# A two-layer graph kernel with its normalised activations made a step ahead, in three buffers, and transposed by one DMA a step, all engine orders rewritten

## The reference

```
h = relu(layernorm(x))                              # over the 256 features
x = x + L0(h, adj, adj, bias)                       # A = adj @ h, C = adj @ h + b,
                                                    # out = max over features of relu(A + (C - A)[..., None])
h = relu(layernorm(x))
x = x + L1(h, ...)                                  # masked attention, 8 heads of 32
```

## Time and profile before

| | us |
|---|---|
| runs of the kernel | 1011.68, 1016.46, 1025.72; median 1016.46 |
| the profiled execution | 1012.4, its span 1010.7 |
| TensorE busy | 817.2 (81% of the span) |
| VectorE busy | 645.9 (64%) |
| ScalarE busy | 489.5 (48%) |
| GpSimd busy | 429.1 (42%) |
| mean granted clock of TensorE | 0.909 of full speed |
| DMA share, mean rate | 120 GB/s |

### The profile page before, as it was taken

The page is one execution under the profiler, slowest core; times in us unless marked ns, Lnnn a source line. Parts: engine busy times, 40 slices in busy tenths (PEclk is TensorE's granted clock), DMA queues, the critical chain, the costliest instruction groups (busy, mean ns, idle before and its releaser), DMA issues.

```text
span 1010.7 us, 31246 instructions
## 1 busy us (share of the span) xinstructions
PE 817.2 (81%) x11241; PEld 536.8 (53%) x11241; DVE 645.9 (64%) x1552; ACT 489.5 (48%) x1192; POOL 429.1 (42%) x853
## 2 busy tenths in 40 slices
PE   1578998788789888888987888798888889997862
PEld 0235665455556555555655555565555566654641
DVE  3554776666667666766765666686576677775653
ACT  3334555454455545545554444555454455553441
POOL 5411554344454434434544343454334445542343
PEclk9788998899999989989998998999899899998885
DMA  4466564667655676676556767555677755655313
GB/s 122 91 143 140 119 130 107 133 137 142 127 99 134 126 128 133 142 148 109 116 127 121 131 137 147 100 125 127 118 138 134 129 122 132 131 117 95 81 23 42
DMA packets 168295, 121.34 MB, mean 120 GB/s; under 512 B 84720, under 2 KB 167408, under 8 KB 167664
## 3 DMA queue, kind: packets, MB, share of 16 engines
q1 hardware_dynamic: 67328, 69.72, 27.2%
q10 hardware_dynamic: 83952, 33.04, 20.8%
q0 software_dynamic: 16896, 16.78, 11.2%
HBM read 35.06 MB, written 33.55 MB: 68 GB/s over the span
## 4 chain that ended last, share of the span: by engine, by line
PE 63%; DMA 17%; issue 9%; DVE 3%; SPq 3%; ACT 3%; POOL 2%; ACTq 1%; DVEq 0%; POOLq 0%
PE a_ps L319 20%; DMA hT<-h_lo 15%; PE sum_ps L446 8%; PE sc_ps L396 6%; PE pv_ps L416 6%; PE sum_ps L419 4%; PE a_ps L304 4%; PE sc_ps L368 4%; PE sc_ps L344 4%; SPq L273 2%; PE a_ps L332 2%; PE sum_ps L443 2%; ACT o_sb L590 1%; PE pv_ps L431 1%; ACTq L533 1%
## 5 line engine op out<-in xcount | busy, mean ns | idle before, releaser
L319 PE MATMUL a_ps<-hT,w_hi 128*128 128x512 f16 x512 | 170.6, 467 | 96.0 <-DMA hT<-h_lo 94.6
L844 POOL TENSOR_TENSOR oT_lo<-oT,oT_hi 128x256 f16<-128x256 f32 x128 | 84.6, 670 | 297.4 <-ACT oT_hi L584 297.3
L673 DVE TENSOR_REDUCE smax<-sc_ps 128x4 f32<-128x512 f32 x256 | 163.7, 681 | 51.7 <-PE sc_ps L368 51.6
L561 ACT ACTIVATE pairs<-a_ps 128x512 f16<-128x512 f32 x128 | 77.8, 608 | 231.1 <-PE a_ps L319 231.1
L665 DVE TENSOR_TENSOR pairs<-a_ps,pairs 128x512 f16<-128x512 f32 x128 | 87.3, 682 | 125.8 <-ACT pairs L561 125.8
L319 PEld LDWEIGHTS a_ps<-hT,w_hi 128*128 128x128 f16 x512 | 53.6, 115 | 168.2 <-issue 113.5
L838 POOL TENSOR_TENSOR h_lo<-h_sb,h_hi 128x256 f16<-128x256 f32 x128 | 89.1, 698 | 116.9 <-ACT h_hi L524 116.5
L571 ACT ACTIVATE p_sb<-sc_ps 128x512 f32<-128x512 f32 x256 | 137.1, 610 | 1.0 <-PE sc_ps L396 0.9
L578 ACT ACTIVATE pv_sb<-pv_ps 128x256 f32<-128x256 f32 x128 | 50.5, 394 | 146.2 <-issue 97.4
L416 PE MATMUL pv_ps<-p_sb,v_sb 128*32 128x128 f32 x2048 | 107.2, 278 | 6.1 <-ACT pv_sb L578 2.6
L723 DVE SCALAR_TENSOR_TENSOR t_sb<-o_sb,mv,w_sb 128x256 f32<-128x256 f32 x128 | 70.1, 586 | 60.9 <-POOL w_sb L869 60.9
(11 more groups left out here) (105 smaller groups left out, 1545.0 us busy)
## 6 DMA issues: line engine op xcount, KB each, us to landing
stack<-pairs SPq DMA_DIRECT2D x768, 64.0 KB, 2.0
out<-in_x SPq DMA_DIRECT2D x32, 512.0 KB, 4.2
out<-y_sb POOLq DMA_DIRECT2D x32, 512.0 KB, 8.4
x_sb<-in_x ACTq DMA_DIRECT2D x31, 512.0 KB, 3.6
stack<-crow SPq DMA_DIRECT2D x64, 8.0 KB, 1.9
w_sb<-in_L_gnn_w_qkv SPq DMA_DIRECT2D x1, 768.0 KB, 7.1
x_sb<-in_x SPq DMA_DIRECT2D x1, 512.0 KB, 3.7
hT<-h_hi ACTq DMA_TRANSPOSE x32, 6.3
```

The lines of the kernel that those rows point to most:

```text
L319: mm = nc.tensor.matmul(a_ps[c % 2][:].rearrange("p (b n) -> p b n", b=G), w[:, dc, col:col + P], hT[:, par, part, :, dc], start=(k == 0), ...
L673: nc.vector.tensor_reduce(smax[:, HC * j:HC * (j + 1), b], sc_ps[u % SC_SLOTS][:], AX.X, ALU.max).then_inc(smax_ready, 1)
L844: nc.gpsimd.tensor_tensor(oT_lo[:, b], oT[:, b], oT_hi[:, b], ALU.subtract).then_inc(olo_ready, 1)
```

## The change

h_hi and h_lo become two halves of one tile `h_parts` with three buffers (`SLOTS`), so what H0 waits for lies two steps further back. One DMA transposes both halves (16 blocks of 128 x 128 in place of 8 and 8), and `hT_in` counts 16 a step. x is normalised two groups ahead of the projections instead of one (a new flag, `norm`), with `rstd1` and `shift1` in three buffers, and it is loaded three groups ahead instead of two; the set-up normalises group 1 and loads group 2 before the pipeline starts. The orders of all five engines are rewritten.

```diff
-        h_hi = sb("h_hi", [P, G, D], F16)
-        h_lo = sb("h_lo", [P, G, D], F16)
+        h_parts = sb("h_parts", [P, SLOTS, 2, G, D], F16)
...
-                step(t, t % SLOTS, t < STEPS, 1 <= t <= STEPS, 2 <= t <= STEPS + 1, t >= 3, t + 1 < STEPS, t + 2 < STEPS)
+                step(t, t % SLOTS, t < STEPS, 1 <= t <= STEPS, 2 <= t <= STEPS + 1, t >= 3, t + 1 < STEPS, t + 2 < STEPS,
+                     t + 3 < STEPS)
...  SyncE
-            ORDER = ("Q0 M0 C0 Q1").split()
+            ORDER = ("C0 Q0 M0 Q1").split()
...  TensorE
-                    pe.wait_ge(hT_in, 32 * (t + 1))
+                    pe.wait_ge(hT_in, 16 * (t + 1))
...
-            ORDER = ("K0 S0 S1 S2 R0 S3 Q0 Q1 R1 N0 E0 E1 E2 L0 R2 E3 O0 R3 K1 S4 O1 L1 S5 S6 O2 S7 O3 Q2 M0 N1 E4 E5 "
-                     "P0 P1 E6 E7 P2 P3 Q3 P4 P5 V0 P6 P7 V1").split()
+            ORDER = ("K0 S0 S1 R0 S2 Q0 S3 R1 Q1 N0 E0 R2 O0 E1 E2 E3 L0 O1 R3 K1 S4 S5 O2 S6 S7 L1 O3 N1 M0 E4 E5 E6 "
+                     "P0 P1 Q2 P2 P3 Q3 P4 P5 E7 V0 P6 P7 V1").split()
...  ScalarE
-            def h_high(t, b):
+            def h_high(t, par, b):
                 act.wait_ge(h_ready, G * t + b + 1)
                 if b == 0:
-                    wait(act, a_psum, 2 * t)
-                    wait(act, hT_in, 32 * t)
-                nc.scalar.activation(h_hi[:, b], h_sb[:, b], ACT.Copy).then_inc(hhi_ready, 1)
+                    wait(act, a_psum, 2 * (t - 2))
+                    wait(act, hT_in, 16 * (t - 2))
+                nc.scalar.activation(h_parts[:, par, 0, b], h_sb[:, b], ACT.Copy).then_inc(hhi_ready, 1)
...
-                for part, h in enumerate((h_hi, h_lo)):
-                    nc.scalar.dma_start_transpose(hT[:, par, part].rearrange("p b c n -> p (b c) n"),
-                                                  h[:].rearrange("p b d -> p (b d)")).then_inc(hT_in, 16)
+                nc.scalar.dma_start_transpose(hT[:, par].rearrange("p a b c n -> p (a b c) n"),
+                                              h_parts[:, par].rearrange("p a b d -> p (a b d)")).then_inc(hT_in, 16)
...
                 wait(act, h_ready, G * (t - 2))
+                act.wait_ge(x_loaded, 16 * t)
                 nc.scalar.dma_start(x_sb[:, par], xg[t]).then_inc(x_loaded, 16)
...
-            ORDER = ("Q0 C0 X0 Q1 C1 E0 E1 E2 E3 C2 O0 C3 O1 R0 R1 H0 O2 R2 O3 H1 M0 H2 R3 A0 Q2 E4 E5 E6 A1 H3 E7 Q3 "
-                     "A2 T0 A3 V0 L0 V1").split()
+            ORDER = ("C0 Q0 R0 R1 C1 Q1 E0 C2 O0 E1 E2 E3 H0 O1 X0 C3 R2 O2 H1 H2 O3 R3 M0 H3 E4 A0 T0 Q2 A1 E5 Q3 E6 "
+                     "E7 A2 V0 A3 V1 L0").split()
...
-                        load_x(t + 2, (k + 2) % SLOTS)
+                        load_x(t + 3, k)
...  VectorE
-            ORDER = ("I0 I1 I2 S0 O0 S1 S2 S3 Q0 O1 X0 X1 O2 O3 Q1 L0 B0 S4 S5 B1 B2 S6 S7 B3 G0 M0 L1 F0 Q2 F1 Q3 F2 "
+            ORDER = ("I0 I1 I2 S0 O0 S1 S2 S3 O1 Q0 O2 X0 Q1 L0 B0 O3 S4 B1 S5 S6 S7 B2 B3 M0 X1 G0 L1 Q2 F0 Q3 F1 F2 "
                      "F3").split()
...
-                            stats_x(t + 1, (k + 1) % SLOTS)
+                            stats_x(t + 2, (k + 2) % SLOTS)
...  GpSimd
-            ORDER = ("C0 C1 X0 C2 C3 H0 H1 N0 H2 W0 W1 W2 H3 W3 K0 D0").split()
+            ORDER = ("C0 C1 C2 H0 C3 H1 H2 H3 N0 W0 W1 W2 W3 K0 D0 X0").split()
...
-                        invert_std_x(t + 1)
+                        invert_std_x(t + 2, (k + 2) % SLOTS)
```

More of the change, by code:

```diff
@@ L228, in pipeline @@
                 for k in range(SLOTS):
-                    step(t + k, (k + 1) % SLOTS, True, True, True, True, True, True)
+                    step(t + k, (k + 1) % SLOTS, True, True, True, True, True, True, True)
             for t in range(STEPS - SLOTS - 1, STEPS + SLOTS):
@@ L273, in stack_heads, with step @@
                         nc.sync.dma_start(dst.rearrange("p s b n -> p s (b n)"), src).then_inc(stacked[j], 16)
-            ORDER = ("Q0 M0 C0 Q1").split()
-            def step(t, k, a, sc, e, d, prep, load):
+            ORDER = ("C0 Q0 M0 Q1").split()
+            def step(t, k, a, sc, e, d, prep, norm, load):
                 for what in ORDER:
@@ L297, in _, with layer0 @@
             pe.wait_ge(dve_const, 3)
-            def layer0(t, i):
+            def layer0(t, par, i):
                 pe.wait_ge(qkhi_ready, 4 * t + i + 1)
                 pe.wait_ge(qklo_ready, 4 * t + i + 1)
-                for k, (w, h) in enumerate(((adjT_hi, h_hi), (adjT_hi, h_lo), (adjT_lo, h_hi))):
-                    mm = nc.tensor.matmul(a_ps[i][:], w[:], h[:, 2 * i:2 * i + 2].rearrange("p b d -> p (b d)"),
+                for k, (w, h) in enumerate(((adjT_hi, 0), (adjT_hi, 1), (adjT_lo, 0))):
+                    mm = nc.tensor.matmul(a_ps[i][:], w[:], h_parts[:, par, h, 2 * i:2 * i + 2].rearrange("p b d -> p (b d)"),
                                           start=(k == 0), stop=(k == 2))
@@ L819, in carry_waits, with invert_std_x @@
                 nc.gpsimd.tensor_tensor(pool_cell[:, cell:cell + 1], pool_cell[:, 0:1], pool_cell[:, 0:1], ALU.add)
-            def invert_std_x(t):
+            def invert_std_x(t, par):
                 pool.wait_ge(mv1_ready, G * (t + 1))
-                wait(pool, h_ready, G * t)
+                wait(pool, h_ready, G * (t - 2))
                 carry_waits(1)
```

44 lines of the change are left out of this document (24 added, 20 removed).

## The result

The changed kernel takes 872.11 us (median of four, 871.38 to 874.03), the kernel before in the same session 1015.54 (1011.68 to 1025.72). The ratio is 0.858, with an interval of 0.851 to 0.864. The profiled execution of after has a span of 869.7 us, 141.0 less than before, at a mean granted clock of 0.957. Ratios set fast executions against fast ones; the kernel before also has slower ones (up to 1040 us, at granted clocks down to 0.889), which are left out of them.

A forecast was written before the change was run, and what follows sets the result against it. TensorE was taken as the bound, its waits for hT the largest loss: from 1012.4 us, -127 for waits and clock, +45 new stalls, +12 clock and fill gave 942, forecast as 946 us for the median; range 895 to 990.

The forecast's parts named there:

- The 81.8 us: TensorE's 24 waits for hT at Q0, without the first fill; all were to go.
- 45.6 less 9 us, 37 net: Slow matmuls behind hT waits: 24 x 1.9 us removed; 9 us returned, one step in five losing 1.65.
- thin stretch: The transpose's new place: DMA share read as 0.31 there, so a landing of 5.5 to 8 us.
- new stalls: Stalls the new order brings to TensorE: 28 x (0.6 + 0.3 + 0.7), put at 45 us.
- I = 3.2 us: Time the joined transpose's issue holds ACT's queue, taken nearest to the sum of two issues.
- the term of 17 us: TensorE's stall at P4 behind ACT's hold, 0.6 us in each of 28 steps.
- 0.3 + 0.7 us a step: Stall at N1 for row maxima, 0.3; thin margins of POOL's X0 and SP's second twelve stack transfers, 0.7.
- The 26.9 us at the back-edge stay.: Seven issue waits at L339, the loop body's first matmul, were to stay, with slow matmuls behind them.
- no cost: SP's copy of x, moved from behind M0 to the step's front, was to cost nothing.
- nothing new stalls: Rival: hold at or below 2.6 us, maxima and stack in time; 897 us, chance 0.15.
- ACT's hold as the new wait: Rival: hold above 4 us, P4 stalls 1.6 and the clock falls; 979 to 1011 us, chance 0.14.
- The stack was late: Rival: SP's second twelve transfers late, TensorE waits 3.8 us at K1 or S4 each step; 1086 us, chance 0.08.

The follow-up runs named there:

- e13: Kernel before with only SyncE's order changed, the copy of x moved to the front of the step: 968.1 us, 0.966.
- e15: Changed kernel with SyncE's old order alone, copy of x behind M0 and the transpose still early: 872.5 us, 0.871.
- e6: Kernel before without the transposes behind step 2 and without the waits for them: 931.5 us, 0.928.
- e3: Changed kernel with the single transpose issued behind A2 again, as before, and not behind A0: 890.7 us, 0.881.
- e10: Changed kernel with the transpose behind A2 and SyncE's old order, the copy of x behind M0: 975.4 us, 0.961.
- e9: Changed kernel with TensorE's O1 put back behind S4 and not ahead of K1: 902.7 us, 0.891.
- e11: Changed kernel with the old orders of four engines and only SyncE's new one: 925.3 us, 0.915.

## Why the prediction was wrong

**What held.** TensorE was the bound and hT its largest wait. The 81.8 us are gone (80.9 with the fill, which grew by 0.9), and the landing in the new place is 6.0 us, within the 5.5 to 8 expected. The slow clock behind the waits was sized at 45.6 less 9 us, 37 net; busy time fell by 51.6. ScalarE's L516 waited for `shift` only once, for 9.0 us at the start, and the waits at L339 for row maxima are 2.8 us in three, none of them in a step of the loop. What was not so is the reason given for the landing: the new place is no thin stretch (share 0.65 in 456.5 to 462.5 us, where 0.31 was read), and the wait is gone because 9.9 us lie between the issue and Q0.

**Where it failed.** Taken from the spans, term by term: hT waits and fill -80.9 (forecast -81.8 + 3), clock -51.6 (forecast -37), new stalls +17.5 (forecast +45), back-edges -11.7 (forecast 0), `take_o` at L443 -10.7, from 13.2 to 2.5 (not in the sum). That is -137.4 of the measured -141.0, against -70. The step that failed is the sum of new stalls and its clock; two more terms that were put at nothing also moved.

1. *The hold of one transpose, I = 3.2 us.* It is 1.88 in the median and 1.44 at the least. I had the row that pointed to it, 1.34 for 8 blocks in the first step, and let the mean of 3.5 from the loop outweigh it. Those holds were measured with the copy beside them: with the copy in front (e13), even the old double issue has medians of 1.27 and 1.64, where it had 1.85 and 1.72. Inside the loop P4 stalls over 0.8 us in four steps, not in 28; the term of 17 us measured 7.2. Nor did the clock follow: behind the stall of 1.57 us it stayed at 1.00.
2. *Thin margins, 0.3 + 0.7 us a step.* The two places named, row maxima and stack, cost 1.3 and 1.9 us more than before, where 28 were put down. What is new instead is P0's wait for M0's chain (10.3 us), which the prediction did not name. I had summed the stalls of several places for every step although each had a lower end of 0.
3. *"The 26.9 us at the back-edge stay."* They became 15.2, in which the transposes no longer run beside them. With the early T0 or without transposes the seven stalls take 15 to 17 us, wherever the copy stands (15.2 in after, 15.6 in e15, 15.4 in e6). With T0 late they take 17.6 (e13) or 21.5 (e3), and with the copy ahead of it 30.1 (e10). How full the DMA engines are does not settle it: at a share of 1.38 a stall of e13 took 2.41 us, at 1.21 one of before took 4.35. Why, stays open.
4. *`take_o`.* The many short waits of 0.4 us at L443 stood in the trace of before, and I did not ask what the new order of O0 to O3 does to them. Putting one O back (e9) costs 30.6 us, 10.5 of it in these waits.

**The copy, "no cost".** For the change as made this is right: with the early T0 its place is worth 0.4 us. As a view of the kernel before it was the largest miss. There the copy makes the issue hold longer, the landing later (6.4 us against 5.5) and the back-edge dearer, and moving it alone gives 34 to 47 us. I named the full stretch (share 1.30) but didn't ask which transfer filled it, and then took prices from that stretch to another place.

**The rivals.** The first, nothing new stalls, at 897, was nearest, and too high as well: it lacked points 3 and 4 and a part of the clock. ACT's hold as the new wait appears only with two or four issues (883, 1036). The stack was late only twice in the first steps and once, for 0.4 us, near the end (6.5 us in 3), though in the old orders it was the next bound (e6).

What stays open: e9 shows that O1's place matters, not how the remaining orders share the 35 us between 925 (e11) and 891 (e3); why the transposes lengthen the stall at the back-edge; and why a stall of 1.57 us left the clock up in after, where one of 1.62 in before and one of 2.14 in after did not.

## What to carry to other kernels

When a stretch of the DMA engines is full, find the one large transfer in it and try moving that first; a price read beside it (an issue's hold, a landing, a stall at the back-edge) need not hold elsewhere. When two edits both take a transfer out of the same crowd, test them as a table of four, since each alone may carry all of it. And a sum of "thin margin" stalls, each of which may be zero, is no forecast of the time but an upper end.

## What the runs showed of the hardware

- A DMA transpose issued by ScalarE holds its queue for about 1.3 us (medians 1.31 and 1.38) whether it has 4 or 8 blocks of 128 x 128, and for 1.65 to 1.88 in the median with 16. A 512 KB copy from HBM to HBM issued just ahead (0.8 us in the step shown) made that 2.75 in the median (3.59 in that step), and the landing 7.1 instead of 5.1 us. Cutting the copy to 16 KB undid both; a copy issued 3.7 us behind the transpose changed neither (1.87 and 6.1).
- TensorE's stall at the loop's back-edge is longer with the transposes beside it: 2.2 us each with them elsewhere or left out, 3.1 with them beside it, 4.3 with the copy ahead of them too (15.2, 21.5 and 30.1 us in seven). The copy alone did nothing (15.4 and 15.6), and the share of the DMA engines does not settle it: 2.41 us were seen at 1.38 (e13) and 4.35 at 1.21 (before). A body of six steps has stalls of 3.0 us, one of three 2.2.
- After a stall of 2.14 us at the back-edge six matmuls took 2.56 us instead of 1.29, the pace of 1.2 GHz; after the stalls of 0.38 us at P0, and after one of 1.57 us at P4, the granted clock stayed at 1.00.
